# A second PSUM bank for one of eight accumulations in an audio tower kernel

## The reference

```python
h = tok(x)                        # 4 small tanh layers, a strided convolution: 16 x 375 x 64
h = h + retention(norm(h))        # rotary queries and keys, decayed scores
h = h + product_key_attention(norm(h))
h = h + one_step_trained_mlp(norm(h))
h = h + mixture_of_experts(norm(h))
```

```python
k = jnp.einsum('bnhk,bnhkd->bnhd', kv_scores, keys_table[ind])
v = jnp.einsum('bnhk,bnhkd->bnhd', kv_scores, values_table[ind])
```

## Time and profile before

| | |
|---|---|
| median of 3 runs | 6420.99 us |
| profiled execution | 6410.07 us, span 6408.2 us |
| TensorE matmuls (PE) busy | 88% of the span |
| ScalarE (ACT) | 72% |
| VectorE (DVE) | 66% |
| GpSimd (POOL) | 66% |
| one batch in the middle | about 370 us |

### The profile page before, as it was taken

One profiled execution on the slowest core, in us unless ns is written; L12 is line 12 of the kernel. 1 busy time (PEld: TensorE's weight loads), 2 busy tenths in 40 slices (PEclk: granted clock), 3 DMA queues, 4 the chain that ended last, 5 costly groups with the idle time before them and its releaser, 6 DMA issues.

```text
span 6408.2 us, 79708 instructions
## 1 busy us (share of the span) xinstructions
PE 5616.6 (88%) x24704; PEld 3125.1 (49%) x24704; DVE 4242.5 (66%) x13138; ACT 4644.2 (72%) x10889; POOL 4212.2 (66%) x4108
## 2 busy tenths in 40 slices
PE   2599998989989898989989898899989899999977
PEld 1345454545545454454545455454545545454533
DVE  7676766848585784858568484957758485772157
ACT  1577777878777786877778787777778777777833
POOL 0386766858586685958677585867768585777700
PEclk9999999999999999999999999999999999999968
DMA  1111111111111111111111111111111111111100
GB/s 35 37 56 41 50 48 41 56 37 56 42 50 46 47 52 37 56 39 53 46 47 52 40 53 39 53 46 47 52 37 58 38 53 43 49 48 50 45 21 15
DMA packets 93462, 290.42 MB, mean 45 GB/s; under 512 B 17880, under 2 KB 26547, under 8 KB 92781
## 3 DMA queue, kind: packets, MB, share of 16 engines
q1 hardware_dynamic: 92748, 285.25, 13.5%
q10 hardware_dynamic: 288, 0.07, 0.0%
HBM read 280.68 MB, written 4.61 MB: 45 GB/s over the span
## 4 chain that ended last, share of the span: by engine, by line
PE 60%; POOL 16%; ACT 16%; DVE 6%; issue 2%; DMA 0%; SPq 0%; DVEq 0%; ACTq 0%
PE accu L520 26%; POOL dense_w L449 16%; PE dense L528 9%; PE dense L506 7%; ACT dense L910 4%; ACT dense_w L904 3%; PE sims L641 3%; PE work L647 2%; PE work L568 1%; PE work L685 1%; PE dense L494 1%; PE dense L816 1%; PE work L634 1%; PE work L621 1%; PE sims L611 1%
## 5 line engine op out<-in xcount | busy, mean ns | idle before, releaser
L449 POOL TENSOR_TENSOR dense_w<-dense_w,store 128x375 f32<-128x375 f32 x4096 | 4209.8, 1049 | 1868.2 <-ACT dense_w L904 1825.2
L520 PE MATMUL accu<-dense_w,store 128*128 128x375 f32 x8192 | 3321.8, 488 | 182.4 <-POOL dense_w L449 123.4
L910 ACT ACTIVATE dense<-dense 128x375 f32<-128x375 f32 x4096 | 1917.1, 468 | 782.5 <-PE dense L528 540.1
L904 ACT ACTIVATE dense_w<-dense 128x375 f32<-128x375 f32 x4096 | 1962.4, 479 | 218.1 <-PE dense L506 216.5
L520 PEld LDWEIGHTS accu<-dense_w,store 128*128 128x128 f32 x8192 | 1434.8, 194 | 496.1 <-POOL dense_w L449 172.0
L528 PE MATMUL dense<-store,hot 128*128 128x375 bf16 x4096 | 1337.8, 327 | 250.1 <-ACT dense_w L904 248.6
L506 PE MATMUL dense<-store,spread 96*128 96x375 bf16 x4096 | 1348.5, 329 | 13.7 <-ACT dense L910 11.0
L528 PEld LDWEIGHTS dense<-store,hot 128*128 128x128 bf16 x4096 | 394.8, 97 | 1114.6 <-ACT dense_w L904 703.3
L1299 DVE TENSOR_REDUCE store<-picks 125x256 bf16<-125x4096 uint16 x192 | 848.6, 4420 | 6.6
L506 PEld LDWEIGHTS dense<-store,spread 96*128 96x128 bf16 x4096 | 402.1, 98 | 793.8 <-ACT dense L910 560.2
L1294 DVE TENSOR_TENSOR picks<-codes,keys 125x4096 uint16<-125x4096 uint16 x192 | 527.7, 2749 | 7.3 <-ACTq L897 1.9
(11 more groups left out here) (255 smaller groups left out, 6048.1 us busy)
## 6 DMA issues: line engine op xcount, KB each, us to landing
store<-in SPq DMA_DIRECT2D x513, 512.0 KB, 3.3
x_in<-in SPq DMA_DIRECT2D x16, 187.5 KB, 2.4
store<-in SPq DMA_DIRECT2D x1, 2048.0 KB, 8.7
queries_kept<-n3T SPq DMA_DIRECT2D x16, 93.8 KB, 3.4
h_saved<-h SPq DMA_DIRECT2D x16, 93.8 KB
store<-queries_kept SPq DMA_DIRECT2D x16, 93.8 KB, 2.4
store<-h_saved SPq DMA_DIRECT2D x16, 93.8 KB
out<-store SPq DMA_DIRECT2D x16, 93.8 KB
```

The costliest lines, as they stand in the source:

```text
L449: nc.gpsimd.tensor_tensor(dense_w[:, i % RING, :], dense_w[:, i % RING, :], first_of[:, i // CHUNKS, :], ALU.mult).then_inc(s["weighed"], 1)
L520: last = mm(accu[:, 0, 0:S], table[:, n % PIECE_RING, i % PIECE, :], dense_w[:, i % RING, :], start=(c == 0), stop=(c == CHUNKS - 1))
L904: fn(dense_w[:, i % RING, :], dense[:, ORDER.step[i] % BANKS, 0:S], ACT.Relu, scale=-1.0).then_inc(s["taken"], 1)
L910: fn(here, here, ACT.Relu, scale=FAR).then_inc(s["past"], 1)
```

## The change

Head 3 of each batch accumulates in `work[:, 0]` instead of `accu`, and is copied from there. The first matmul of head 3 then waits for the copy of head 1 instead of head 2, and the first matmul of head 4 for that of head 2 instead of head 3; both are long done. The other heads stay as they are. An assertion says that head 3's slots lie in the rounds of picking.

```diff
+ROUNDS_AT = EARLY + sum(FILL_PREPARE) + sum(FILL_GRADIENT)
+LENT_TO = 3
+assert ROUNDS_AT <= LENT_TO * CHUNKS + SUM_LAG and (LENT_TO + 1) * CHUNKS + SUM_LAG <= EARLY + AHEAD
...
+        summed_in = [accu[:, 0, 0:S], work[:, 0, 0:S]]
...
                     if c == 0 and h >= 1:
-                        pe.wait_ge(s["acc_done"], b * H + h)
+                        pe.wait_ge(s["acc_done"], b * H + h - (h in (LENT_TO, LENT_TO + 1)))
                     pe.wait_ge(s["weighed"], i + 1)
-                    last = mm(accu[:, 0, 0:S], table[:, n % PIECE_RING, i % PIECE, :], dense_w[:, i % RING, :],
+                    last = mm(summed_in[h == LENT_TO], table[:, n % PIECE_RING, i % PIECE, :], dense_w[:, i % RING, :],
                               start=(c == 0), stop=(c == CHUNKS - 1))
...
-                    nc.scalar.copy(kvT[:, h, :], accu[:, 0, 0:S]).then_inc(s["acc_done"], 1)
+                    nc.scalar.copy(kvT[:, h, :], summed_in[h == LENT_TO]).then_inc(s["acc_done"], 1)
```

## The result

| | before | after |
|---|---|---|
| median of 4 runs each | 6417.88 us (6412.18 to 6425.69) | 6373.27 us (6368.22 to 6382.01) |
| ratio, 95% interval | | 0.9926 (0.9913 to 0.9938) |
| profiled execution | 6410.07 us, span 6408.2 us | 6373.58 us, span 6371.8 us |
| mean granted clock of the profiled execution | 0.974 | 0.977 |
| time with the clock at its low level, per batch (mean of 14) | 11.95 us | 9.06 us |

The change gains 44.6 us between the medians and 36.5 us between the profiled executions. The forecast was a gain of 23. The last row of the table is the sum of the stretches in which the trace has the granted clock at half, that is at 1.2 instead of 2.4 GHz.

What follows compares the result with a forecast made beforehand. TensorE's accumulation and GpSimd's weighting were taken to limit the kernel in turns. Gains of 14.3 + 6.8 + 2.2 = 23.3 us gave a forecast median of 6398 us, likeliest 6390 to 6405, range 6373 to 6420.

Steps and rivals of the forecast that it cites:

- Part 1: Start of head 4: 1.08 us freed, 0.95 us a batch carried on, 14.3 us for 15 batches.
- only whole steps are carried: GpSimd's run after head 4's start: comparisons let it carry only whole steps, so 0.95 of 1.08 us.
- GpSimd's second run in batch 2: Sign: the run of some 46 steps should begin 1.1 to 2 us earlier after the last L736.
- Part 2: Start of head 3: 1.08 us freed, 0.45 us a batch kept (bounds 0 and 0.95), 6.8 us for 15 batches.
- Part 3: Last batch, no picking beside it, TensorE sets the pace: both handovers kept whole, 2.2 us.
- Cover for ScalarE's copy: At the handovers: 0.2 us of cover keeps the copy from delaying TensorE; cost taken as 0, at most 12 us.
- rival B: Low-clock stretches vanish with shorter stalls: a gain of 32 to 50 us, 6371 to 6389; chance 0.15.
- Rival A: GpSimd takes the freed time back at the comparisons: gain 0 to 12 us, 6409 to 6421; chance 0.22.
- Rival C: Low-clock stretches come in all batches instead of every second one: 21 us slower, 6442; chance 0.06.
- Rival D: Head 3's first step finds another wait, GpSimd's weighting, in the same place: nothing moves, 6421; chance 0.05.
- L520 <- issue: Sign in TensorE's waits: this group of the accumulation's stalls should lose 32 of them.
- L526 starts every 0.95 us: Sign: the accumulation should start every 0.95 us across both handovers, with ScalarE's copy beside it.

Runs made afterwards that it cites:

- the second comparison: The changed kernel, unaltered, run again on another occasion and chip: 6367.19 us against 6427.87 for the kernel before, ratio 0.99.
- wait4_only: Kernel before with head 3 in the work bank and only head 4's wait relaxed: 6403.02 us, ratio 0.9975.
- bank_only: Kernel before with head 3 in the work bank and every wait as before: 6423.46 us, ratio 1.0003.
- after_q1: Changed kernel with one query matmul of the attention repeated once: 6407.97 us, ratio 0.9997; on another occasion 6366.46 us, ratio 0.9911.
- before_warmA: Kernel before with twelve unused matmuls filling the idle ahead of head 3, no wait removed: 6402.23 us, ratio 0.9973.
- before_q3: Kernel before with one query matmul of the attention repeated three times: 6424.98 us, ratio 1.0017.

## Why the prediction was right or wrong

The side was right and the two freed waits did what was told; the size was wrong. 6398 was forecast and 6373 measured, a miss of 25 us. Some 3 us of it are the kernel before itself, 6417.88 us in this comparison instead of 6420.99. **The step that failed is the clock**: the sum has no term for it. The places of the two waits gave 24.2 us between the profiled executions (17.1 + 7.1) against 23.3 forecast, and everything else gave 12.3 where the sum has nothing.

**Part 1, head 4: right, a little small.** Forecast 0.95 us a batch, measured 1.06 (steps 127 to 129: 2.97 to 1.91), all of it kept to step 190. The step of my argument that failed is "only whole steps are carried". Head 4 began earlier against head 3 and steps 129 to 190 took the same (72.75 against 72.76 us, mean of 14 batches), and GpSimd's second run in batch 2 took 53.23 us for 46 steps against 53.20. So the comparisons took the same time from the run and not a whole step more or less. The Trainium skill's rule that I leaned on (GPSIMD Engine Reference, 8. Key points: GpSimd and VectorE contend for SBUF interfaces) says that the two get in each other's way; that the gain comes in whole steps was my own addition, and the trace refutes that.

**Part 2, head 3: right on average, by a mixture.** Forecast 0.45 us a batch; between the two profiled executions steps 90 to 127 fell from 43.40 to 42.97, by 0.43. Behind it stand three sizes. Where the clock is full the gain is 0.13 or 0.14 us, well under the 0.3 to 0.5 that I took from GpSimd's pause of 0.28 us. Where a low stretch begins 5.6 to 6.1 us behind step 90 it is some 0.46 us (between the means), and where it begins later and reaches into the head it is 0.68, with the stretch itself shorter. The prediction had both of these as "about 0.5 us, or more if the stretch itself gets shorter". That the mean came out so near is partly luck: it hangs on how many batches are of which kind.

**Part 3, the last batch: right.** Steps 90 to 127 took 35.27 us instead of 36.32, so that head 3's wait was kept nearly whole, and head 4's start came 30.50 us behind head 3's (5861.46 to 5891.96) instead of 31.56 us (5896.35 to 5927.91), 1.06 us: 2.1 us against 2.2.

**The waits together.** At the full clock throughout they would give 16 x 1.06 + 15 x 0.14 + 1.05 = 20 us by the starts; with the shorter low clock at head 3 it was 24.2, against 23.3 forecast. By whole runs at equal clock it is 28.4 and 30.8 us in the two comparisons of the changed kernel, and 3.7 + 21.7 = 25.4 by its parts. The difference to the starts is left open. Cover for ScalarE's copy, taken at nothing: right, as its timeline shows.

**The clock: the term that was missing.** I priced it as rival B, with 0.15, and left it out of the sum. Between the two profiled executions the low clock fell from (1 - 0.974) x 2 x 6408.2 = 333 us to (1 - 0.977) x 2 x 6371.8 = 293 us. By the slope of the 97 runs 0.003 is 12 us, as much as the 12.3 us outside the two handovers. Between the medians the share is larger (44.6 less 28.4, 16 us), and in the second comparison 60.7 less 30.8, 30 us. So forecast and rival B were both at work at once, while I had priced them as cases that exclude each other. The reason that I gave for B, shorter stalls at the handover, holds for a part. At head 3 the freed stall halves the late stretches, from 6.8 to 3.4 us, in every batch that has one. Steps 90 to 127 hold 1.95 us less of low clock in a batch, of 2.89 less in all; what that gave in time is in the 7.1 us already. The low clock doesn't begin by the stall: in front of it is the idle of 2.27 us for ScalarE's exponentials, as long after the change as before. Why there is less low clock in steps 0 to 90 and 224 to the next 0, far from both handovers, and in which batches it follows the idle of 2.27 us, was not found. Since one program alone moves by as much from one occasion to the next, it isn't shown either that these 12 us belong to the change.

Rival A (GpSimd takes it back) is refuted at head 4 and mostly true at head 3 where the clock is full (0.93 of 1.07 us). The sentence of the Trainium skill behind it (TensorE: Matmul & The Clock Gate, HAM oscillation: a second PSUM buffer "gave no further gain") does not describe this kernel: wait4_only against bank_only is a second buffer for one handover, and it gained 20 us. Rival C, slower by the clock, did not come, but after_q1's first comparison, with 15.55 us of low clock per batch and no gain at all, shows that it had a right to its place. Rival D is refuted by bank_only beside the changed kernel: 16 stalls at `work` with the wait, none without.

**My signs.** "L520 <- issue" lost 31 stalls, 32 were foretold: the 32 are gone and one came at head 5. L526 starts every 0.95 us across head 4's handover in all 16 batches, and across head 3's in 9; in the other seven the low clock makes one or both of its steps 1.25 to 1.88 us. GpSimd's second run in batch 2 was to begin 1.1 to 2 us earlier behind the last L736. It began 0.36 us earlier (1075.13 for L742 to 1154.48, 79.35 us; before 1075.02 to 1154.73, 79.71), and L627 came at 1203.53 instead of 1203.76. That sign was wrong for this batch because of the low clock from 1101.81, which the same batch of before doesn't have. One batch that is disturbed by the clock is no sign; the mean over batches is.

## What to carry to other kernels

A wait for a copy out of a PSUM bank costs the idle and the slower step behind it, here 1.08 us. What freeing it gives can be forecast from the timeline to within a few tenths of a microsecond by asking which engine sets the pace behind it. Where GpSimd's next run began behind a pause of 1.71 us that TensorE and ScalarE set, all of it was kept (1.06 us at head 4). Where GpSimd's pause was 0.28 us, less than that pause was kept (0.14 us at head 3, at the full clock). Then add the granted clock as a term of its own with a wide range, and not as a rival. Sort the batches by their low clock before their times are averaged. Compare time and mean granted clock of every run before a gain below 0.5% is put down to an edit, and repeat it on a second occasion.

## What the runs showed of the hardware

- **The same program differs by its granted clock.** 97 executions of one program on five chips spread over 39 us, 0.6%, and on one chip alone over up to 32 us, with a correlation of -0.96 between time and mean granted clock. after_q1 had 0.9705 on one chip and 0.9775 on another, 6407.97 and 6366.46 us.
- **A stall inside a low stretch kept the clock low.** With head 3's stall of 1 us the late stretches last 6.8 us in 23 of 23 batches, without it 3.4 us in 30 of 30.
- **Low clock can cost nothing.** In steps 129 to 190, where GpSimd works without a gap for 53 us, a batch takes 72.74 to 72.78 us with a low stretch of 3.4 us and 72.71 to 72.78 without.
- **Less idle, more clock, at one place.** With twelve dead matmuls in an idle of 2.27 us there was no low clock behind it in any of 14 batches; the kernel ran 19.1 us faster, and between the profiled executions some 7 of 13 us lay at this place. The Trainium skill (TensorE: Matmul & The Clock Gate, HAM oscillation) lays the loss to idle between bursts of matmuls; before_warmA agrees, with the clock of 12 us around the place at 1.00 instead of 0.72. The waits on that page take 3 to 5 us; here the longest single idle at the place is 2.27 us, and the low clock follows it in some batches only.
- **More work can be nearly free in one execution.** before_q3 does 1.32 us more in each batch, and two batches take 740.62 instead of 740.66 us, with less low clock. At equal clock it costs 18 us in all.
- **GpSimd beside VectorE gave no rounding to whole steps.** 1.06 us gained ahead of a run that VectorE's comparisons slow down was 1.06 us behind it.
